# A fused block of two routed layers and an attention: the order of the instructions around each batch's attention stretch

## The reference, cut to what matters

```python
def ffn(x, w_router, w_block):                 # on each batch alone
    k = int(1024 * 0.75)
    scores = einsum('bld,d->bl', x, w_router)
    _, top_idx = top_k(scores, k)
    processed = gelu(selected @ w_block)       # the k best tokens
    return x.at[batch_idx, top_idx].set(processed)

def attn(x):                                   # 16 heads of 32, causal
    q = (x @ Wq.T) in heads;  latent_k = x @ Wk_down.T;  latent_v = x @ Wv_down.T   # 64 wide
    logits = einsum(einsum(q, q_to_latent), latent_k) / 8
    return (softmax(causal(logits)) @ latent_v, times v_up) @ Wout.T

x = x + 0.5 * ffn(layernorm(x))
x = x + attn(layernorm(x))
x = x + 0.5 * ffn(layernorm(x))
```

## Time and profile before

| | before |
|---|---|
| median of 3 runs | 2327.71 us (2326.27 to 2329.19) |
| the profiled execution | 2326.99 us, of which the span is 2325.1 us |
| TensorE busy | 2153.9 us, 93% of the span |
| VectorE busy | 1760.4 us, 76% |
| ScalarE busy | 1101.7 us, 47% |
| GpSimd busy | 488.9 us, 21% |
| mean granted TensorE clock | 0.974 of full speed |

### The profile page before, as it was taken

One profiled execution on the slowest core, in us unless ns is written; L12 is line 12 of the kernel. 1 busy time (PEld: TensorE's weight loads), 2 busy tenths in 40 slices (PEclk: granted clock), 3 DMA queues, 4 the chain that ended last, 5 costly groups with the idle time before them and its releaser, 6 DMA issues.

```text
span 2325.1 us, 52505 instructions
## 1 busy us (share of the span) xinstructions
PE 2153.9 (93%) x21256; PEld 1314.2 (57%) x21256; DVE 1760.4 (76%) x5017; ACT 1101.7 (47%) x1942; POOL 488.9 (21%) x574
## 2 busy tenths in 40 slices
PE   5589999999999999999999999999999999999997
PEld 4454477545775456744667446764466544775446
DVE  5668857887678876798677886788857888578747
ACT  2335643456425554255543565435643456435562
POOL 2201212114112231023210232111221113121132
PEclk8789999999999999999999999999999999999999
DMA  4300021210212103021021210211111120212000
GB/s 140 145 1 32 9 73 40 104 42 2 91 55 74 38 14 98 37 74 38 20 91 38 74 39 24 87 44 69 39 58 52 55 93 3 73 37 74 2 2 37
DMA packets 71934, 123.16 MB, mean 53 GB/s; under 512 B 2832, under 2 KB 33040, under 8 KB 67600
## 3 DMA queue, kind: packets, MB, share of 16 engines
q1 hardware_dynamic: 71696, 119.81, 14.8%
HBM read 81.53 MB, written 37.75 MB: 51 GB/s over the span
## 4 chain that ended last, share of the span: by engine, by line
PE 78%; DVE 12%; ACT 5%; issue 4%; POOL 1%; DMA 0%; DVEq 0%; POOLq 0%; SPq 0%; ACTq 0%
PE psum L860 29%; PE psum L873 18%; PE psum L994 11%; PE psum L1001 10%; PE psum L876 5%; DVE part L1143 3%; ACT pr L840 2%; PE psum L887 2%; DVE psum L1145 2%; PE psum L912 2%; DVE junk L1095 1%; DVE junk L1093 1%; DVE qk L1132 1%; PE psum L918 1%; ACT nt_h L746 1%
## 5 line engine op out<-in xcount | busy, mean ns | idle before, releaser
L840 ACT ACTIVATE pr<-psum 128x512 f32<-128x512 f32 x1152 | 617.8, 597 | 525.2 <-PE psum L876 525.0
L873 PE MATMUL psum<-qk,qk 32*128 32x512 f32 (+3 forms) x4608 | 515.3, 370 | 60.6 <-DVE part L1143 22.8
L1145 DVE CUSTOM_DVE_ANT_0 psum<-psum,mask_b 128x512 f32<-128x512 f32 (+3 forms) x1024 | 472.8, 521 | 105.5 <-PE psum L887 103.5
L873 PEld LDWEIGHTS psum<-qk,qk 32*128 32x128 f32 x4608 | 318.5, 186 | 384.0 <-ACT pr L840 337.5
L887 PE MATMUL psum<-qk,qk 32*128 32x512 f32 (+3 forms) x4608 | 511.7, 370 | 20.6 <-DVE part L1143 19.1
L1143 DVE TENSOR_REDUCE part<-psum 128x1 f32<-128x512 f32 x512 | 325.0, 681 | 54.7 <-PE psum L887 52.2
L887 PEld LDWEIGHTS psum<-qk,qk 32*128 32x128 f32 x4608 | 311.0, 186 | 43.0 <-DVE part L1143 22.9
L994 PE MATMUL psum<-pr,v_sb 128*32 128x512 f32 (+3 forms) x3072 | 314.6, 504 | 2.3 <-ACT ht L746 1.6
L1001 PE MATMUL psum<-pr,ones 128*32 128x512 f32 (+3 forms) x3072 | 306.4, 494 | 0.0
L738 POOL TENSOR_SCALAR_AFFINE_SELECT pr<-pr 128x512 f32<-128x512 f32 x256 | 162.0, 654 | 558.4 <-ACT pr L840 556.3
L860 PE MATMUL psum<-wb_h,nt_h 128*128 128x512 f32 x512 | 208.0, 406 | 10.9 <-DVE wb_l L1042 7.0
(11 more groups left out here) (116 smaller groups left out, 3368.0 us busy)
## 6 DMA issues: line engine op xcount, KB each, us to landing
nt_raw<-x_turned_dram SPq DMA_DIRECT2D x16, 1024.0 KB, 6.1
x<-x_dram SPq DMA_DIRECT2D x16, 1024.0 KB, 7.1
spill_x<-x SPq DMA_DIRECT2D x16, 1024.0 KB, 4.7
x<-spill_x SPq DMA_DIRECT2D x16, 1024.0 KB, 6.9
out_dram<-x SPq DMA_DIRECT2D x14, 1024.0 KB, 4.9
w_h<-scratch_o SPq DMA_DIRECT2D x28, 256.0 KB, 3.0
w_l<-scratch_o SPq DMA_DIRECT2D x28, 256.0 KB, 3.3
w_h<-scratch_q SPq DMA_DIRECT2D x6, 1024.0 KB, 4.9
```

Of the source, the lines that this page charges most:

```text
L840: nc.scalar.activation(pr_of(b, g, u)[:, 2 * p + place, :], bank(e, place), ACT.Exp, scale=SCALE).then_inc(exp_ready, 1)
L873: eng.matmul(o, (k_h, k_h, k_l)[t][own, P * j:P * (j + 1)], (q_h, q_l, q_h)[t][own, queries], start=(t == 0 and at == 0), stop=False, skip ...
L1145: m = nc.vector.tensor_tensor_reduce(scores, scores, mask_b[:, BANK - w:BANK], 1.0, FAR, ALU.add, ALU.max, top_of)
```

## The change

The list `sched` is rearranged in five places, and one group of matmuls is issued in another way.

1. In the opening, statistics and dots stand before the weights' work and the layer tiles, all eight ranks follow the score row, and the query weights are split before the output weights, which get buffers of their own.
2. K and V are issued as a pair, their six matmuls in turns.
3. Values and denominators of the stretch stand one chunk earlier.
4. The old batch's layer tiles 6 and 7 and its ranks 2 to 6 move from the first group to `back(b)`; only rank 7 stays, in chunk 0, and the weave of `RF`, `GX` and `CB` starts at chunk 1 in place of 3.
5. These two layer tiles take banks of the ring.
6. In the closing, layer tile 5 goes before the second score row.

```diff
@@ opening
-        out = [("WC", 0)] + sum([raw(0, i) for i in range(TC)], []) + [("WS", 0)]
+        out = sum([raw(0, i) for i in range(TC)], [])
         for c in range(NC):
             for i in range(TC * c, TC * (c + 1)):
                 out += stats(0, 0, i)
             out += scales(0, 0, c)
-        out += sum([raw(0, i) for i in range(TC, NT)], [])
-        for i in range(TC):
+        out += [("WC", 0), ("WS", 0)] + sum([raw(0, i) for i in range(TC, NT)], [])
+        for i in range(NT):
             out += dot(0, 0, i)
-        out += layer(0, 0, 0) + layer(0, 0, 1)
-        for i in range(TC, NT):
-            out += dot(0, 0, i)
...
+        out += layer(0, 0, 0) + layer(0, 0, 1) + [("SC", 0, 0, 0), ("SC", 0, 0, 1), ("WS", 1), ("WS", 2)]
+        out += [("RT", 0, 0, i) for i in range(NT)]
+        for i in range(2, NT):
+            out += layer(0, 0, i)
+        out += [("RF", 0, 0)] + [("GX", 0, 0, i) for i in range(NT)]
+        out += summed(0, 0) + summed(0, 1) + summed(0, 2) + summed(0, 3)
+        out += [("VA", 1, 0, 0), ("RS", 1, 0, 0), ("WS", 3), ("NM", 1, 0, 0)]
...
+        out += [("LAT", 0, 0), ("XS", 0, 0), ("NO", 1, 0, 4), ("NO", 1, 0, 5), ("K", 0, 0, 0), ("V", 0, 0)]
+        out += [("Q", 0, 0, 0), ("WS", 4), ("T", 1, 0, 4), ("NO", 1, 0, 6), ("T", 1, 0, 5), ("NO", 1, 0, 7)]
...
+        out += [("XL", 1, 0), ("XL", 1, 1), ("K", 0, 0, 1), ("V", 0, 1), ("Q", 0, 0, 1)]
+        beside = [[("Q", 0, 1, 1)], [("K", 0, 1, 0), ("V", 0, 2)], [("K", 0, 1, 1), ("V", 0, 3)], [("Q", 0, 2, 0)],
+                  [("Q", 0, 2, 1)], [("Q", 0, 3, 0)], [("Q", 0, 3, 1)], [("K", 0, 2, 0), ("V", 0, 4), ("K", 0, 2, 1), ("V", 0, 5)]]
...
+        out += [("K", 0, 3, 0), ("V", 0, 6)] + turned(0, 0, 0)
+        return out + [("K", 0, 3, 1), ("V", 0, 7)]
@@ project
-        out += [("Q", b, 0, 0), ("Q", b, 1, 0), ("K", b, 0, 0), ("T", 1, b, 4), ("NO", 1, b, 6)]
+        out += [("Q", b, 0, 0), ("Q", b, 1, 0), ("K", b, 0, 0), ("V", b, 0), ("T", 1, b, 4), ("NO", 1, b, 6)]
...
-        out += [("Q", b, 0, 1)] + loads[0] + keys[1] + [("V", b, 0)] + splits[0] + [("V", b, 1)] + splits[1]
+        out += [("Q", b, 0, 1)] + loads[0] + keys[1] + [("V", b, 1)] + splits[0] + splits[1]
@@ attention
-            groups[g].append(combined(n, 0) + (then(n - 3, "HR") if n >= 3 else []) + (values(n - 2) if n >= 2 else []))
+            groups[g].append(combined(n, 0) + (then(n - 3, "HR") if n >= 3 else []) + (sums(n - 2) if n >= 2 else []))
             groups[g].append(combined(n, 1) + (then(n - 3, "HE") if n >= 3 else []) + mask(n) + [("MC", *e) for e in closes(n)]
-                             + ([("XT", *e) for e in closes(n - 1)] if n else []) + (sums(n - 2) if n >= 2 else []))
+                             + ([("XT", *e) for e in closes(n - 1)] if n else []) + (values(n - 1) if n >= 1 else []))
         last = len(units) - 1
-        return groups, [then(last - 2, "HR") + then(last - 2, "HE") + values(last - 1), sums(last - 1), values(last),
+        return groups, [then(last - 2, "HR") + then(last - 2, "HE") + sums(last - 1), values(last), [],
                         sums(last) + then(last, "HR") + then(last, "HE")]
@@ back
-        out += layer(1, b, 4) + [("RT", 1, b, 0), ("RT", 1, b, 1)] + layer(1, b, 5)
+        out += [("RT", 1, b, 0), ("RT", 1, b, 1)] + layer(1, b, 4) + [("RT", 1, b, 2), ("RT", 1, b, 3)] + layer(1, b, 5)
+        out += [("RT", 1, b, 4), ("RT", 1, b, 5)] + layer(1, b, 6) + [("RT", 1, b, 6)] + layer(1, b, 7)
@@ closing
-        out += dot(1, b, 3) + layer(1, b, 4) + turn(3) + [("SC", 1, b, 0)] + layer(1, b, 5)
+        out += dot(1, b, 3) + layer(1, b, 4) + turn(3) + layer(1, b, 5) + [("SC", 1, b, 0)]
@@ the first group of the stretch
-            groups[0][0] += [("F", 1, b - 1, 6), ("RT", 1, b - 1, 2), ("RT", 1, b - 1, 3)]
-            groups[0][1] += [("F", 1, b - 1, 7), ("G", 1, b - 1, 6), ("G", 1, b - 1, 7), ("RT", 1, b - 1, 4), ("RT", 1, b - 1, 5)]
-            groups[0][2] += [("RT", 1, b - 1, 6)]
-            groups[0][3] += [("RT", 1, b - 1, 7)]
+            groups[0][0] += [("RT", 1, b - 1, 7)]
...
-            groups[0] = [weave(groups[0], tail, 3, len(groups[0]) // 2 + 3)]
+            groups[0] = [weave(groups[0], tail, 1, len(groups[0]) // 2 + 2)]
@@ banks
-        elif k == "F" and e[3] >= 6 and e[2] + 1 < B:
-            own = banks[e] = [e[3]]
@@ TensorE, K with V
+                    for t, (w, l) in enumerate([(wkv_h, lat_h), (wkv_h, lat_l), (wkv_l, lat_h)]):
+                        m = eng.matmul(bank(e), w[0:L, P * g:P * (g + 1)], l[0:L, c * BANK:(c + 1) * BANK],
+                                       start=(t == 0), stop=(t == 2))
...
+                        m = eng.matmul(bank(v), l[L:P, P * i:P * (i + 1)], w[L:P, :], start=(t == 0), stop=(t == 2))
```

More of the change, by code:

```diff
@@ L130, in opening @@
             out += scales(0, 0, c)
-        out += sum([raw(0, i) for i in range(TC, NT)], [])
-        for i in range(TC):
+        out += [("WC", 0), ("WS", 0)] + sum([raw(0, i) for i in range(TC, NT)], [])
+        for i in range(NT):
             out += dot(0, 0, i)
-        out += layer(0, 0, 0) + layer(0, 0, 1)
-        for i in range(TC, NT):
-            out += dot(0, 0, i)
-        out += [("SC", 0, 0, 0)] + layer(0, 0, 2) + [("SC", 0, 0, 1)] + [("RT", 0, 0, i) for i in range(3)] + [("WS", 1)]
-        out += [("RT", 0, 0, i) for i in range(3, 6)] + layer(0, 0, 3) + [("WS", 2)] + [("RT", 0, 0, 6), ("RT", 0, 0, 7)]
-        out += [("RF", 0, 0)] + [("GX", 0, 0, i) for i in range(NT)] + [("WS", 3)] + layer(0, 0, 4) + layer(0, 0, 5)
-        out += layer(0, 0, 6) + layer(0, 0, 7)
-        out += summed(0, 0) + summed(0, 1) + summed(0, 2) + summed(0, 3) + scales(1, 0, 0) + [("WS", 4)]
+        out += layer(0, 0, 0) + layer(0, 0, 1) + [("SC", 0, 0, 0), ("SC", 0, 0, 1), ("WS", 1), ("WS", 2)]
[5 more added lines that the diff above has]
+        out += [("VA", 1, 0, 0), ("RS", 1, 0, 0), ("WS", 3), ("NM", 1, 0, 0)]
         out += [("NO", 1, 0, 0), ("NO", 1, 0, 1)]
@@ L154, in opening @@
             out += turned(0, 0, 1) if u == 8 else []
-        out += [("V", 0, 5), ("V", 0, 6), ("V", 0, 7), ("K", 0, 2, 0), ("K", 0, 2, 1)] + turned(0, 0, 0)
-        return out + [("K", 0, 3, 0), ("K", 0, 3, 1)]
+        out += [("K", 0, 3, 0), ("V", 0, 6)] + turned(0, 0, 0)
+        return out + [("K", 0, 3, 1), ("V", 0, 7)]
     def project(b, left):
@@ L332, in program_order @@
             taken.add(after)
+    for e, after in zip(sched, sched[1:]):
+        if e[0] == "K":
+            assert after[0] == "V"
+            beside[e] = after
     return sched, beside
@@ L386, in macaron @@
         k = e[0]
-        if e in beside_of:
+        if e in beside_of and k != "V":
             continue
@@ L437, in macaron @@
         for one in (e, beside.get(e)):
-            if one:
+            if one and (one == e or one[0] != "V"):
                 for place, n in enumerate(banks[one]):
@@ L476, in macaron @@
         prs = [over(f"pr{n}", region[n], [P, SLOTS, HQ, BANK]) for n in range(3)]
-        raw_b, raw_o, raw_q = (over(f"raw_{w}", region[0] + 8192 * n, [P, NK, E]) for n, w in enumerate("boq"))
+        raw_b, raw_q = over("raw_b", region[0], [P, NK, E]), over("raw_q", region[0] + 16384, [P, NK, E])
+        raw_o = over("raw_o", region[1], [P, NK, E])
+        wo_h, wo_l = over("wo_h", region[1] + 8192, [P, NK, E], F32R), over("wo_l", region[1] + 16384, [P, NK, E], F32R)
         raw_lat = over("raw_lat", region[0] + 24576, [P, NK, P])
@@ L808, in _ @@
                     act.wait_ge(q_done, nth[e])
+                    if b == 0 and g >= 2:
+                        act.wait_ge(scr_out, 64)
                     if b:
@@ L937, in _ @@
                     b, g, c = e[1:]
-                    pe.wait_ge(split, 10)
+                    pe.wait_ge(split, 8)
                     if b >= 2:
@@ L947, in _ @@
                     pe.wait_ge(latl_ready, nth["LAT", b, c])
-                    passes(bank(e), (wkv_h, wkv_l), (lat_h, lat_l), 1, lambda w, n: w[0:L, P * g:P * (g + 1)],
-                           lambda t, n: t[0:L, c * BANK:(c + 1) * BANK]).then_inc(k_done, 1)
-                elif k == "V":
-                    b, i = e[1:]
+                    v = beside[e]
+                    i = v[2]
                     pe.wait_ge(latl_ready, nth["LAT", b, i // TC])
-                    passes(bank(e), (lat_h, lat_l), (wkv_h, wkv_l), 1, lambda t, n: t[L:P, P * i:P * (i + 1)],
-                           lambda w, n: w[L:P, :]).then_inc(v_done, 1)
+                    for user in before[v]:
+                        pe.wait_ge(*freed(*user))
+                    for t, (w, l) in enumerate([(wkv_h, lat_h), (wkv_h, lat_l), (wkv_l, lat_h)]):
+                        m = eng.matmul(bank(e), w[0:L, P * g:P * (g + 1)], l[0:L, c * BANK:(c + 1) * BANK],
+                                       start=(t == 0), stop=(t == 2))
+                        if t == 2:
+                            m.then_inc(k_done, 1)
```

(3 more changed lines are left out.)

19 lines of the change are left out of this document (6 added, 13 removed).

## The result

The changed kernel takes 2351.92 us (2347.68 to 2356.1, 4 runs) against 2326.99 us (2323.08 to 2329.19) for the kernel before on the same chip: ratio 1.0106, 95% interval 1.0087 to 1.0124. It is 25 us, or 1.1%, slower. The forecast was 2344 us, slower, with a range of 2312 to 2356. Its profiled execution took 2356.1 us, span 2354.1 us, mean granted clock 0.966.

The account below looks back on a forecast made before the run. TensorE, busy 93% of the span, was taken as the bound, with VectorE's chain binding the opening. Costs of 35.7 less gains of 18.5 us net +17: 2326.99 + 17.2 = 2344 us, own range 2334 to 2354, overall 2312 to 2356.

Parts of the forecast that it names:

- Values a chunk ahead: End of the stretch: values 34 wait 3.2 us for a mask behind eight GX, seven batches, +22.4 us.
- The clock behind the new wait: End of the stretch: low clock of 3.4 us after the mask wait, two times in three, +7.7 us.
- The same values out of the projection: Projection: values leaving it give back only about 0.6 of 1.43 us before the latent projection, +5.6 us.
- The head: Start of each stretch: layer tiles and ranks moved out, 0.5 us gained in each of seven, -3.5 us.
- Banks: Last two layer tiles using banks the first scores take, every other batch: counted as nothing.
- K and V: Projection: V 0 rides with the first K, saving 0.7 us in each of seven batches, -4.9 us.
- Rival 4: Projection: side-by-side issue saves 0.7 us in all 64 K and V pairs, 45 us, giving 2304; chance 0.03.
- The opening: Before the first scores: shorter VectorE chain, GX from 55.0, first turned tile 5.8 us earlier, sum -8.5 us.
- The closing: End of the kernel: scores 35 fill the 1.64 us wait of values 34 for ScalarE's copy, -1.6 us.
- Inside the stretch: Within the groups: masks and exponentials ready in 3.6 of 3.95 us, so no wait, 0 (bounds +-7).

Follow-up runs that it names:

- Masks first: The changed kernel with the next batch's eight GX moved on GpSimd behind the mask of unit 34: 2318.99 us, ratio 0.9962.
- six-GX run: The changed kernel with six of the eight GX ahead of the mask of unit 34 and two behind it: 2328.58 us, ratio 1.0014.
- part 3 alone: The kernel before with only the stretch's values and denominators one chunk earlier: 2346.16 us, ratio 1.0085.
- without part 3: The changed kernel with values and denominators where they stood before: 2329.04 us, ratio 1.001.
- the kernel before with values and masks: The kernel before with values and denominators a chunk ahead and GX behind the mask of unit 34: 2314.63 us, ratio 0.9953.

## Why the prediction was right, and where it was not

- *Values a chunk ahead.* Right in place, mechanism and size: one mask behind eight GX. 22.4 us forecast, 19.8 measured: one wait of 3.29 us and six of 2.75, where I had taken the upper end, 3.2, for all. Masks first and the six-GX run show that GpSimd's queue is the cause.
- *The clock behind the new wait.* 7.7 us forecast; the end stage of the changed kernel is 231.9 - 201.9 = 30.0 us longer than with masks first, so 10.2 beside the waits. The clock fell in four of seven, with 6.8 us in two of them, 20.4 us in all at half speed. With part 3 alone it fell in all seven; how often it falls was a guess (two in three) that came out near. The sum of both terms, 30.1, was met.
- *The same values out of the projection.* 5.6 us forecast. The latent projection's wait grew by 0.9 us in every batch, from 0.41 or 0.50 to 1.30 or 1.40, so the cause is right. In the three batches where no other wait differs, the end stage is 28.20 us before and 28.45 with masks first, and it holds 0.45 us less work (the values of unit 33): the cost is 0.7 us, where 0.8 was forecast. In the other four a wait ahead of a layer tile gets 0.5 to 0.7 us shorter, which I did not see. The whole stage is 1.1 us shorter with 3.2 us less work in it, so the term came to about +2.

```profile
327.34 0.47 PE L865 MATMUL psum<-nt_h,wlat_h 128*128 128x512 f32 x1 [1.40 <-DVE nt_l L1079]
```

- *The head.* This is the step that failed. -3.5 us forecast (bounds -17.5 and +3). From first rank to second values the seven heads take 178.9 us before, with a chunk of 1.1 us more in each, so 171.2; part 3 alone makes that 161.0, and the changed kernel 174.9. Moving the layer tiles out thus costs some 2 us a head, 14 in all, and without part 3 it costs as much (178.9 to 195.2). So the loss is not that two parts act on one place: this term had the wrong sign by itself. In batch 3 I had four chunks done 18.3 us after the first rank (18.2 before); with masks first it is 20.0. I counted only gaps behind VectorE's maxima and put ScalarE at nothing. In the new head TensorE waits 1.5 to 1.7 us before the first two chunks, for ScalarE in all but two 0.82 us waits that have no releaser on record, and 0.7 us more for it in six heads; its idle is 4.0 us a head, where 3.8 were forecast and 3.4 stood before. I had written that the clock most likely falls here again: it does, in all seven, but for longer (51 us against 44), where the old head with part 3 has 17.
- *Banks.* "I count nothing" was wrong twice: a wait of 0.8 to 1.0 us in every second head, which only covers another, and a gain of 4.9 us of waits and some 3 of clock at the first tiles of the output projection, far from the edit. In the stage table the new head costs 1524.8 - 1508.3 = 16.5 us in the stretch, some 4 of them an issue gap with its low clock, and gives 8.6 back here; the medians differ by 9.8.
- *K and V.* 0.7 us a batch: right on the trace. Rival 4 gave nothing more: pairs that were neighbours ran side by side before. The Trainium skill, "TensorEngine Tiling (Array Packing)", Key Properties, says that different tiles can load and multiply in parallel; the traces agree, with starts 0.01 us apart.
- *The opening.* -8.5 us forecast, of which -1.5 was for batch 0's head, which the table has in "stretch"; -3.7 measured against the other -7.0. GX start at 56.31 (60.14 before; 55.0 forecast). The first turned tile came 3.8 us earlier where 5.8 were forecast, and the stages behind it, where TensorE now waits 1.2 to 2 us several times, gave nothing of the further 1.2 us.

```profile
68.55 1.94 PE L917 MATMUL psum<-ident,norm 128*128 128x128 f32 x8 [13.89 <-ACT norm L768]
```

- *The closing.* -1.6 us forecast; 69.5 to 67.9, so -1.6. The wait of 1.64 us is gone, as forecast. The values of unit 33 (0.45 us) have left this stage too, and a wait of 0.33 us ahead of the output projection is new in it, so the exact match is partly luck.
- *Inside the stretch.* 0 forecast (within 7). In the kernel before with values and masks the stretch is 7.2 us shorter, with 3.2 us of work more in it: from first scores to second values 20.0 to 21.0 us fell to 17.6, of which 1.1 came back later as moved work. So values ahead gave some 10 us that I had at nothing, nearly all of it in the heads, where the clock then stays up.

The sum, on the profiled executions: 17.2 us forecast, 29.1 measured (2356.1 - 2326.99; the medians differ by 24.9). Wait and clock of part 3 came out right (30.1 and 30.0), the 5.6 was 3.6 too much, the K, Q stage gave 4.3 more than forecast, and head, stretch and opening, forecast at -12, came to +7.7. Of this, some 9 us are the two stops with nothing on record that holds TensorE, which no term had. So the verdict rests on the right cause, while the nearness of the total is in part luck: the head's +14 and values ahead's -10 were both missed, and cancel.

## What to carry to other kernels

Before moving a consumer ahead, find the queue of the engine that produces for it and see what was only harmless there while the consumer was late: here eight GX ahead of one mask cost 30 us, and swapping two events turned a loss of 1.1% into a gain of 0.4%. Work that fills TensorE between waits is worth more than its own time when the clock falls without it: compare idle and busy time of the stretch apart, since equal idle with more busy time for the same matmuls was the clock's sign here. And where banks are handed out by a ring, count the takes: two more or fewer in each batch changed the waits some 220 us further on by 5 us.

## What the runs showed of the hardware that was not expected

In the first group of some batches TensorE stops for about 2 us while nothing that the profile shows holds it. Twice in the changed kernel; here in batch 3, TensorE and then the DMA of 1024 to 1036 us:

```profile
1032.52 0.27 PE L1005 MATMUL psum<-pr,v_sb 128*32 128x128 f32 x1 [2.18 <-issue]
...
1033.34 0.69 PE L878 MATMUL psum<-qk,qk 32*128 32x512 f32 x2
```

```profile
DMA  9999999999989999999999999999710000000001
...
q1 hardware_dynamic: 1547, 3.07, 73.8%
q8 instruction: 2, 0.03, 1.0%
```

The DMA engines are at nine tenths for eight of these twelve microseconds with the batch's loads and stores of x, and two packets of instructions are fetched in the same time. Behind the stop the clock falls (0.69 us for a pair that takes 0.50). The two stops of the changed kernel, with the clock behind them, make its first groups 5.2 and 3.9 us longer than before. Stops of 1.5 us and more stand in four of the kernels with the new head, at five places in the first groups of batches 1, 3 and 6, and in none with the old head. That the instructions came late because of the loads is a reading from the coincidence: no run moved the loads to test it.

Why the kernel's low-clock time outside the edited places changes from run to run of different kernels (83 to 94 us between two whose edit is worth 0.7 us a batch) stays open.
